# Vision block on one core: the expert mask as a VectorE product with choices spread by DMA, and filters made a period ahead

## The reference

```python
y = relu(bn(conv1_w · x)); wdyn = conv2_w · y + conv2_b      # 9 filter values per pixel
h = sum_k unfold3x3(x)[k] * wdyn[k]                          # (b, h*w, c)
n = layernorm(h); Q, K, V = n Wq + bq, n Wk + bk, n Wv + bv
h = h + softmax(Q K^T / 8) V
n = layernorm(h); idx = argmax(n router_w^T + router_b)      # one of 32 experts per token
hid = relu(n W1[idx] + b1[idx])                              # 16 wide
h = h + relu(hid W2[idx] + b2[idx])
```

## Time and profile before

| what | us |
|---|---|
| median of three runs | 1156.71 |
| lowest, highest | 1154.79, 1158.39 |
| profiled execution, its own time | 1155.53 |
| its span from first to last instruction | 1153.6 |
| TensorE busy in the span | 1108.8 |
| ScalarE busy | 630.7 |
| VectorE busy | 491.2 |

### The profile page before, as it was taken

One profiled execution on the slowest core, in us unless ns is written; L12 is line 12 of the kernel. 1 busy time (PEld: TensorE's weight loads), 2 busy tenths in 40 slices (PEclk: granted clock), 3 DMA queues, 4 the chain that ended last, 5 costly groups with the idle time before them and its releaser, 6 DMA issues.

```text
span 1153.6 us, 29604 instructions
## 1 busy us (share of the span) xinstructions
PE 1108.8 (96%) x12890; PEld 632.6 (55%) x12890; DVE 491.2 (43%) x1101; ACT 630.7 (55%) x698; POOL 11.2 (1%) x34
## 2 busy tenths in 40 slices
PE   6597999999999999999999999999999999999996
PEld 2132576666654565665656566555655555555542
DVE  6788726437255280724526272552503030311323
ACT  2355465564646465564656556564655645555551
POOL 3000000000000000000000000000000000000000
PEclk9999899999999999999999999999999999999997
DMA  5645323131105220041202121040000000000000
GB/s 149 139 111 129 78 65 68 30 74 29 47 12 117 53 66 2 14 93 38 65 11 59 38 65 39 11 94 10 11 2 11 2 11 1 11 1 11 2 2 20
DMA packets 15349, 51.67 MB, mean 45 GB/s; under 512 B 2846, under 2 KB 6046, under 8 KB 14828
## 3 DMA queue, kind: packets, MB, share of 16 engines
q1 hardware_dynamic: 15212, 49.68, 18.5%
HBM read 41.77 MB, written 4.75 MB: 40 GB/s over the span
## 4 chain that ended last, share of the span: by engine, by line
PE 93%; DVE 2%; DMA 2%; issue 1%; ACT 1%; SPq 0%; DVEq 0%
PE z_ps L664 39%; PE scores L653 37%; PE both L620 4%; PE both L635 4%; PE both L512 2%; PE both L616 1%; DMA filter_ring<-filters 1%; PE both L643 1%; PE both L550 1%; PE both L560 1%; DMA xin<-x_dram 1%; PE both L581 1%; PE both L600 1%; PE both L591 1%; PE both L627 0%
## 5 line engine op out<-in xcount | busy, mean ns | idle before, releaser
L856 ACT ACTIVATE probs<-scores 128x1024 f32<-128x1024 f32 x480 | 465.4, 1021 | 427.2 <-PE scores L653 427.2
L653 PE MATMUL scores<-g_t,keys_t 64*64 64x512 f32 x4096 | 528.7, 593 | 9.8 <-issue 8.5
L664 PE MATMUL z_ps<-probs,keys 64*64 64x512 f32 x4096 | 525.7, 592 | 0.0
L653 PEld LDWEIGHTS scores<-g_t,keys_t 64*64 64x64 f32 x4096 | 251.7, 134 | 209.4 <-issue 179.1
L664 PEld LDWEIGHTS z_ps<-probs,keys 64*64 64x64 f32 x4096 | 234.9, 134 | 158.7 <-issue 136.5
L1107 DVE COPY o_sb<-both 128x512 f32<-128x512 f32 x14 | 9.7, 691 | 322.6 <-PE both L635 322.6
L1007 DVE TENSOR_TENSOR hres<-hres,tap_product 128x504 f32<-128x504 f32 (+1 forms) x128 | 88.9, 694 | 11.2 <-issue 0.9
L1002 DVE SCALAR_TENSOR_TENSOR tap_product<-filter_ring,w,xin 128x504 f32<-128x504 f32 (+1 forms) x120 | 89.0, 742 | 7.0 <-DMA filter_ring<-filters 3.6
L620 PE MATMUL both<-y_t,w 64*64 64x512 f32 x464 | 66.9, 597 | 0.0
L849 ACT ACTIVATE hidden<-both 128x1024 f32<-128x1024 f32 (+1 forms) x58 | 58.5, 1009 | 6.5 <-PE both L620 6.5
L635 PE MATMUL both<-hidden,w 64*64 64x512 f32 x448 | 57.3, 592 | 0.0
(11 more groups left out here) (136 smaller groups left out, 589.8 us busy)
## 6 DMA issues: line engine op xcount, KB each, us to landing
filter_ring<-filters SPq DMA_DIRECT2D x90, 384.0 KB, 5.1
out_dram<-out_sb SPq DMA_DIRECT2D x32, 128.0 KB, 2.4
xin<-x_dram SPq DMA_DIRECT2D x6, 528.0 KB, 9.8
g_t<-g_t SPq DMA_DIRECT2D x24, 128.0 KB, 4.6
hidden<-once_dram SPq DMA_DIRECT2D x1, 930.0 KB, 14.5
hidden<-once_dram SPq DMA_DIRECT2D x1, 576.0 KB, 6.3
filters<-filters_sb SPq DMA_DIRECT2D x30, 18.0 KB
xin<-x_dram SPq DMA_DIRECT2D x1, 384.0 KB, 6.5
```

The source lines that it names most:

```text
L653: last = T.matmul(scores[rows_of(h), c, r * 512:(r + 1) * 512], keys_t[rows_of(r), i // NQ % 2, k * 128 + 64 * h:k * 128 + 64 * h + 64], g ...
L664: last = T.matmul(z_ps[rows_of(c), h, :], keys[rows_of(h), i // NQ % 2, 2 * k + r, :], probs[rows_of(h), (2 * g + c) % RING, r * 512:(r + ...
L856: A.activation(probs[:, unit % RING, :], scores[:, c, :], ACT.Exp, scale=SCALE if n else first_scale[:, 0:1]).then_inc(probs_ready, 1)
```

## The change

Blocks 3 to 13 (`CHOSEN_BY_DMA`, eleven blocks) no longer have the four mask matmuls of each `hid` fill. SyncE stores the turned one-hot (`onehot_t`, bf16) to HBM, waits for it, and loads it back with each expert's row repeated for its 16 hidden rows, as four DMAs to `chosen`. VectorE drains the `hid` fills with one operation on 128x1024: max(place, 0) times `chosen`. ScalarE does not touch them. The layernorm of block i becomes a fill of its own, `ln`; in usual periods it stands in group 7, after `lg`. `ot` moves from 10 to 8, `xt` from 8 to 9, `g` from 9 to 10, `hid0` to `hid3` to 12 to 15 and `o2` to 16. `cc` and `cv` of a pair come one period earlier (block 9's in groups 4 and 16 of period 3; 11, 13 and 15 in periods 5, 7 and 9), and SyncE's order changes with them.

```diff
-NONE = ("sum", "pow", "aw", "part", "z")
+NONE = ("sum", "ln", "pow", "aw", "part", "z")
+CHOSEN_BY_DMA = range(3, BLOCKS - 2)
 def fourth_groups():
-    return {..., 4: at(7, "sum2"),
+    return {..., 4: [*at(9, "cc"), *at(7, "sum2 ln")],
-            14: at(2, "hid3"), 15: at(2, "o2")}
+            14: at(2, "hid3"), 15: at(2, "o2"), 16: at(9, "cv")}
 def usual_groups(n):
-    pair = {4: at(j, "cc"), 7: at(j, "cv")} if j in PAIRED else {}
-    groups = merged({-1: at(m, "z"), 1: at(m - 1, "fin"), 2: at(m, "pz"), 4: at(i, "sum2"), 5: at(m, "yt"), 6: at(m, "lg")}, pair,
-                    {8: at(i, "xt"), 9: at(i, "g"), 10: [*at(m, "ot"), *at(j, "sum0 sum1")]})
-    if n < BLOCKS - 1:
-        return merged(groups, {11: at(m, "hid0"), 12: at(m, "hid1"), 13: at(m, "hid2"), 14: at(m, "hid3"),
-                               15: at(m, "o2")})
+    pair = {4: at(j + 1, "cc"), 7: at(j + 1, "cv")} if j + 1 in PAIRED else {}
+    groups = merged({-1: at(m, "z"), 1: at(m - 1, "fin"), 2: at(m, "pz"), 4: at(i, "sum2"), 5: at(m, "yt"),
+                     6: at(m, "lg"), 7: at(i, "ln")}, pair,
+                    {8: at(m, "ot"), 9: at(i, "xt"), 10: [*at(i, "g"), *at(j, "sum0 sum1")]})
+    if m in CHOSEN_BY_DMA:
+        return merged(groups, {12: at(m, "hid0"), 13: at(m, "hid1"), 14: at(m, "hid2"), 15: at(m, "hid3"), 16: at(m, "o2")})
+            def spread_choices(i):
+                ot = f"ot@{i}"
+                sp.wait_ge(drained[places.of[ot]], places.nth[ot])
+                for c in range(2):
+                    sp.dma_start(choices[i, :, c, :], onehot_t[64 * c:64 * c + E, :]).then_inc(choices_stored, 16)
+                sp.wait_ge(choices_stored, 32 * (i - CHOSEN_BY_DMA[0] + 1))
+                for f in range(FT):
+                    rows = choices[i, f * 128 // H:(f + 1) * 128 // H, :, :].rearrange("e c n -> e (c n)")
+                    sp.dma_start(chosen[:, f, :, :].rearrange("p c n -> p (c n)"),
+                                 rows.unsqueeze(1).broadcast_to([128 // H, H, 2 * 512])
+                                 ).then_inc(choices_loaded, 16)
                 if n > 3:
                     store_block(n - 2)
+                if n == 2:
+                    store_filters(NQ + 3)
                 if n + NQ + 1 < BLOCKS:
-                    if n > 1 and n + NQ + 1 in PAIRED:
-                        store_filters(n + NQ + 1)
-                    spread_filters(n + NQ + 1)
+                    spread_filters(n + NQ + 1, range(CHUNKS - 1))
+                if n > NQ and n + NQ + 2 in PAIRED:
+                    store_filters(n + NQ + 2)
+                if n - 1 in CHOSEN_BY_DMA:
+                    spread_choices(n - 1)
+                if n + NQ + 1 < BLOCKS:
+                    spread_filters(n + NQ + 1, range(CHUNKS - 1, CHUNKS))
                 if n + NQ < BLOCKS:
                     copy_queries(n + NQ)
                 if n in (2, 3):
                     store_block(n - 2)
+                if n == 3:
+                    store_filters(NQ + 5)
     # TensorE, hid fill
-                            T.matmul(mine[rows_of(c), r, :], mask_w[rows_of(r), cols[c]], onehot_t[rows_of(r), :],
-                                     start=True, stop=False)
+                            if i not in CHOSEN_BY_DMA:
+                                T.matmul(mine[rows_of(c), r, :], mask_w[rows_of(r), cols[c]], onehot_t[rows_of(r), :],
+                                         start=True, stop=False)
     # VectorE
+                if name == "ln":
+                    layernorm(i)
+                    return
+                if name.startswith("hid") and i in CHOSEN_BY_DMA:
+                    f, k = int(name[3:]), places.of[full]
+                    dve.wait_ge(choices_loaded, 16 * FT * (i - CHOSEN_BY_DMA[0] + 1))
+                    dve.wait_ge(filled[k], places.nth[full])
+                    V.scalar_tensor_tensor(hidden[:, f, :, :], place[k][:, :, :], 0.0, chosen[:, f, :, :], ALU.max,
+                                           ALU.mult).then_inc(drained[k], 1)
```

More of the change, by code:

```diff
@@ L108, in opening_groups @@
              *at(0, "pow3 pow4 pow5"), *at(3, "cv"), *at(0, "xt g")],
-        0: at(1, "sum0 sum1 sum2"),
+        0: at(1, "sum0 sum1 sum2 ln"),
         3: at(1, "xt"),
-        4: [*at(1, "g"), *at(2, "sum0 sum1 sum2")],
-        HALF: [*at(0, "part"), *at(3, "sum0 sum1 sum2")],
+        4: [*at(1, "g"), *at(2, "sum0 sum1 sum2 ln")],
+        HALF: [*at(0, "part"), *at(3, "sum0 sum1 sum2 ln")],
         10: at(2, "xt"),
@@ L133, in third_groups @@
 def third_groups():
-    return {-1: at(1, "z"), 0: at(0, "lg"), 2: at(0, "ot"), 3: at(1, "pz"), 4: [*at(0, "hid0"), *at(6, "sum2")],
+    return {-1: at(1, "z"), 0: at(0, "lg"), 2: at(0, "ot"), 3: at(1, "pz"), 4: [*at(0, "hid0"), *at(6, "sum2 ln")],
             5: at(0, "hid1"), 6: at(0, "hid2"), 7: at(0, "hid3"), 8: at(1, "yt"), 9: at(0, "o2"), 10: at(1, "lg"),
@@ L140, in fourth_groups @@
 def fourth_groups():
-    return {-1: at(2, "z"), 0: at(1, "hid2"), 1: at(1, "hid3"), 2: at(2, "pz"), 3: at(1, "o2"), 4: at(7, "sum2"),
+    return {-1: at(2, "z"), 0: at(1, "hid2"), 1: at(1, "hid3"), 2: at(2, "pz"), 3: at(1, "o2"), 4: [*at(9, "cc"), *at(7, "sum2 ln")],
             5: at(2, "yt"), 6: at(2, "lg"), 7: at(1, "fin"), 8: at(7, "xt"), 9: at(7, "g"),
             10: [*at(2, "ot"), *at(8, "sum0 sum1")], 11: at(2, "hid0"), 12: at(2, "hid1"), 13: at(2, "hid2"),
-            14: at(2, "hid3"), 15: at(2, "o2")}
+            14: at(2, "hid3"), 15: at(2, "o2"), 16: at(9, "cv")}
 def usual_groups(n):
     m, i, j = n - 1, n + NQ, n + NQ + 1
-    pair = {4: at(j, "cc"), 7: at(j, "cv")} if j in PAIRED else {}
-    groups = merged({-1: at(m, "z"), 1: at(m - 1, "fin"), 2: at(m, "pz"), 4: at(i, "sum2"), 5: at(m, "yt"), 6: at(m, "lg")}, pair,
-                    {8: at(i, "xt"), 9: at(i, "g"), 10: [*at(m, "ot"), *at(j, "sum0 sum1")]})
-    if n < BLOCKS - 1:
-        return merged(groups, {11: at(m, "hid0"), 12: at(m, "hid1"), 13: at(m, "hid2"), 14: at(m, "hid3"),
-                               15: at(m, "o2")})
+    pair = {4: at(j + 1, "cc"), 7: at(j + 1, "cv")} if j + 1 in PAIRED else {}
[4 more added lines that the diff above has]
+        return merged(groups, {12: at(m, "hid0"), 13: at(m, "hid1"), 14: at(m, "hid2"), 15: at(m, "hid3"), 16: at(m, "o2")})
     return groups
@@ L199, in vit_block_kernel @@
     filters = nc.dram_tensor("filters", (BLOCKS, HH, TAPS, BT * W), F32).ap()
+    choices = nc.dram_tensor("choices", (BLOCKS, E, 2, 512), BF16).ap()
     plan = whole_plan()
@@ L236, in vit_block_kernel @@
         onehot_t = sb("onehot_t", [128, 512], BF16)
+        chosen = sb("chosen", [128, FT, 2, 512], BF16)
         hidden = sb("hidden", [128, FT, 2, 512])
@@ L362, in store_filters, with spread_filters @@
                                      ).then_inc(filters_stored, 16)
-            def spread_filters(i):
+            def spread_choices(i):
[9 more added lines that the diff above has]
+                                 ).then_inc(choices_loaded, 16)
+            def spread_filters(i, parts=range(CHUNKS)):
                 sp.wait_ge(filters_stored, filters_stored_with(i))
-                for part in range(CHUNKS):
+                for part in parts:
                     slot, before = slot_of(i, part)
@@ L620, in fill @@
                             last = T.matmul(mine[rows_of(c), r, :], w1[rows_of(r), cols[c]], y_t[rows_of(r), :],
-                                            start=False, stop=True)
+                                            start=i in CHOSEN_BY_DMA, stop=True)
                     last.then_inc(done, 1)
@@ L1059, in drain @@
                             filters_used[slot] if t == CHUNK - 1 else None)
-                    if part == CHUNKS - 1:
-                        layernorm(i)
                     return
```

3 lines of the change are left out of this document (2 added, 1 removed).

## The result

In six runs each on one chip the changed kernel has a median of 1146.47 us (1142.41 to 1149.97), the kernel before 1155.75 (1153.89 to 1158.39): a ratio of 0.992, interval 0.9896 to 0.9944, or 6.5 to 12.0 us. Faster by 0.8%, as forecast. Measured again in another job, with 6 runs against 11, the same file gave 0.991 (0.9891 to 0.993).

A forecast was written before the change was run, and what follows sets the result against it. TensorE's steps were taken to bound the middle periods. Mask -9.5, `o2` +0.7, `xt` +0.6 and `cv` +0.5 sum to -7.7, so 1147.8 from 1155.53, forecast as 1148.0 us, range 1145 to 1152.5.

The forecast's parts named there:

- The mask: Mask matmuls removed from TensorE's 44 hidden fills in eleven blocks, 0.216 us each, all on the path: -9.5 us.
- ScalarE's drains at 0: 44 x 1.02 us of drains taken off ScalarE lie beside TensorE's work: price 0.
- The product at 1.23 us: VectorE's added 128x1024 product takes 1.23 us, bounds 1.02 and 2.45; 54 us more on VectorE, hidden beneath TensorE.
- `o2`'s wait: `o2` in group 16 waits for `hid3`'s drain: 1.69 against 1.72 just fits; 0.06 x 11 = +0.7 us, ends 0 and 13.
- The choices at price 0: Store and loads on SyncE land 10 us after `ot` is drained, before `hid0` needs them; cover 5.4 us: price 0.
- `xt`: `xt` waits 0.12 us behind VectorE's layernorm in periods 4, 6, 8, 10, 11: +0.6 us, ends 0 and 5 x 0.5.
- `cv` of block 9: In group 16 of period 3, `cv` waits for VectorE to drain `o2` of block 2: +0.5 us, once.
- Filters a period ahead at 0: Filters made a period earlier end VectorE's wait of 7.13 us, which TensorE didn't notice: gain 0 in the middle.
- The rival of late choices: TensorE waits at `hid1` if choices land beyond 15.4 us after `ot`'s drain; at 20 us, 1197; chance 0.05.
- The clock rival: Each new short wait drops TensorE's clock, next two steps at half speed, eleven blocks lose 38 us: 1184; chance 0.02.
- the 5 us at the top of the range: Allowance in the forecast's upper end for each `o2` waiting 0.3 us, with `xt` and `cv` at their ends.
- the cases that gain: The forecast itself, chance 0.78, and more than the sum, where none of the tight places holds: 1146, chance 0.06.

The follow-up runs named there:

- e1: The kernel before with only the mask matmuls of blocks 3 to 13 left out, so the output leaves out the choice: 1146.28 us, ratio 0.9931.
- e3: The changed kernel with VectorE's product on `hid3` issued twice in each of the eleven blocks: 1158.73 us in its one run.
- e4: The changed kernel with the four choices loads made twice, first into an unused tile, so the choices land later: 1179.7 us in its one run.
- the second profile: A second profile of the same changed kernel, run again unchanged: 1146.62 us (6 runs), ratio 0.991 to the kernel before.
- e6_xt_later: The changed kernel with `xt` in group 10, `g` in 11, and `cv` of block 9 ahead of `o2` of block 2: 1146.71 us, ratio 0.9904.
- e2: The changed kernel's schedule and filters, but masks on TensorE, drain on ScalarE and no choices by DMA: 1157.56 us, ratio 1.001 to the kernel before.
- e5: The changed kernel with `cc`, `cv` and the filter stores back where they were before: 1164.09 us, ratio 1.0064 to the kernel before.

## Why the prediction was right, point by point

**The mask: right.** -9.5 against -9.33 by e1 over the same eleven blocks, and 0.86 a period.

**ScalarE's drains at 0: right.** ScalarE's 44.8 us less moved nothing; e1 keeps its drains and has the same periods 12 to 14 as the changed kernel.

**The product at 1.23 us: right,** with 1.225 in the group above. I had taken it from the SBUF row of 1.226, against the estimate of 1.19 by the Trainium skill (VectorE: DVE Perf Modes, the TRN2 errata section). The trace speaks against that figure: with an operand from PSUM and one in bf16 the operation still takes what the SBUF row takes.

**`o2`'s wait: +0.7 charged, 0.2 measured.** The working was right to a few hundredths: 1.69 against 1.72 in it, and 0.34 + 1.22 + 0.15 = 1.71 in the trace. VectorE did start some hundredths later, and ten of the eleven periods still have no wait. e3 shows that there is 0.1 us of room and no more: made to wait, `o2` follows the product by 0.05, not 0.15. Period 5's 0.23 is a term that the prediction did not have: VectorE's pause, 0.4 us in front of the product.

**The choices at price 0: right, with less room than I wrote.** The cover of 15.4 us is 16.4 by e4 in periods with `xt` and `g`, 0.6 of it because `ot` is drained by the very next ScalarE instruction and not behind two others (the store goes out 1.9 us after `ot` starts, where I had 2.5). The rest is mostly how it is read: a wait in the trace counts from a modelled end, some 0.2 us late, and TensorE follows the product by 0.05 in e4 where I had 0.15. The 10 us held only where nothing else was on the queues. In period 12, SyncE's queue and the windows of its loads (columns as in the earlier trace rows):

```profile
883.61 0.78 SPq L375 DMA_DIRECT2D choices<-onehot_t  x2
886.45 2.54 SPq L380 DMA_DIRECT2D chosen<-choices  x4
```

```profile
889.00:892.00 3.00, 3.00 (x32) 1.68 (x28) 0.00 (x0) 1.50 (x3) 0.00 (x0) 1.00 0.50 192
892.00:895.00 3.00, 3.00 (x32) 1.68 (x28) 0.00 (x0) 1.87 (x2) 0.00 (x0) 1.00 0.24 91
```

Over half of the 1 MB moves at 192 GB/s and the rate has fallen by 892 to 895, some 10 us after the store. In period 4 a third filter chunk, the query copy and an image follow on the same queue:

```profile
353.44 0.78 SPq L375 DMA_DIRECT2D choices<-onehot_t  x2
355.37 2.57 SPq L380 DMA_DIRECT2D chosen<-choices  x4
358.65 1.49 SPq L393 DMA_DIRECT2D filter_ring<-filters  x2
361.89 1.34 SPq L403 DMA_DIRECT2D g_t<-g_t  x2
363.28 1.25 SPq L349 DMA_DIRECT2D xin<-x_dram  x2
```

```profile
368.28 1.22 DVE L1102 SCALAR_TENSOR_TENSOR hidden<-both,chosen 128x1024 f32<-128x1024 f32 x1 [4.50 <-DMA chosen<-choices]
```

There it takes 14.8 us from the store to the first product, VectorE waits 4.50, and some 1.5 us of the cover are left. In the second profile the product of that period starts at 14.5 and waits for TensorE, not for the DMA. I had named the image and the query copy as things queued behind the choices, and not asked whether they would slow what stands in front of them. The term stayed at 0, but "cover 5.4 us" was true of the late periods only.

**`xt`: +0.6, measured about 1.0.** The sum had 5 x 0.12. It was 0.09 in p6 and 0.06 in p11, near the charge, and 0.43 and 0.41 in p8 and p10, near the upper end of 0.5 but not for the reason given (logits late). It is VectorE's pause of 0.45 us without a releaser, which falls into the layernorm there (618.10 and 749.38). The kernel before has such pauses too (269.63 and 634.94 among others), and had no step waiting on them. The upper bound covered the size; I had read no row of it.

**`cv` of block 9: +0.5, measured 0.5.** TensorE after, with the last weighing of period 3, `cv`, and the first score step of period 4:

```profile
316.38 0.60 PE L693 MATMUL z_ps<-probs,keys 64*64 64x512 f32 x2
...
318.62 1.09 PE L588 MATMUL both<-conv,conv_w 64*64 64x512 f32 x8
320.51 1.95 PE L682 MATMUL scores<-g_t,keys_t 64*64 64x512 f32 x16 [0.81 <-issue]
```

The weighing starts at 316.38, so `cv` could have started at 318.10 and did at 318.62. The 0.81 behind it, with "issue", belongs to the loss at the start of period 4 that the other kernels have too. That loss is 1.7 us here, `cv`'s 0.5 included, and 1.4 in the kernel before, so period 4 as a whole is only 0.3 over before's; with `cv` ahead of `o2` it is 0.6 (e6_xt_later).

**Filters a period ahead at 0: the step that was wrong in kind.** As long as one asks what the move gives to the kernel before, it is 0, which e2 shows. But in this change its task is another. With the filters where they were, the choices' store queues behind the filter loads, and e5 loses 17.5 us. I had the line in hand, "the first two chunks now go out before `spread_choices` can hold them", and looked only at what the choices delay, not at what delays them. The rival of late choices named its point, 15.4 us, rightly. It took twice 10 us as its case, at 4.6 us a block; period 8 of e5 has 20.0 and 4.57 (its store goes out 1.1 us late, behind the filters' issues, which takes up the wider cover). What kept the rival from happening was this part of the change.

**The clock rival: a real mechanism that the changed kernel's waits don't set off.** Its waits of up to 0.5 us in front of fills left the granted clock at 1.00, in periods 10 and 11 among others (the windows above). Given waits of some 2 us and more at `hid1`, it is there: ten waits of 1.97 to 6.52 us in e4 and e5, seven falls. I had weighed it at 2 in 100 on the strength of one wait of 1.64 us without a fall, and that reading held. The Trainium skill (TensorE: Matmul & The Clock Gate, the second HAM failure mode) tells of small idles between groups that bring a fall; none came after waits of 1.32 us or less here.

**The sum.** -7.7 forecast; -7.9 by the distances up to period 15 in both profiles, -7.6 and -8.9 to TensorE's last instructions, and -9.3 between the medians, whose interval (-6.5 to -12.0) holds them all. That the small errors cancel, 0.5 too much for `o2` and 0.4 too little for `xt`, is luck. Two slips in the working changed nothing: the 5 us at the top of the range should be 6.3 by its own terms (3.3 + 2.5 + 0.5), and the chances of the cases that gain, 0.78 + 0.06, make less than the 0.85 given to faster.

## What to carry to other kernels

Where one engine is busy throughout, price a change by what leaves that engine, and then walk each new neighbour pair: here a distance of one step (1.72 us) held a drain that ends at 1.56 with 0.1 to spare, and a pause of 0.4 us on the draining engine was enough to break it once. A part of a change that is worth nothing to the old kernel can be what lets the new part work, so ask of every new transfer what is already in its queue, and take the part out to see. And compare by distances between repeated steps before believing a span: here 4.8 of 13 us were chance in the opening.

## What the runs showed of the hardware that I had not expected

- A store of 2 x 32 KB lets the loads behind it go 1.9 us after its issue in most periods (2.4 to 2.8 in two of the changed kernel's, up to 3.8 in other runs), and 6.7 to 8.4 us after it behind four loads of 384 KB issued just before on the same queue (e5).
- VectorE stands for about 0.45 us at fixed places of its program, with no releaser in the profile, in both kernels, and 82 of 85 such pauses have an instruction packet on DMA queue 14 beside them. That it is the cause is not shown. It costs only where a step waits for VectorE: 0.4 us in periods 8 and 10, 0.2 in period 5.
- The clock doesn't follow the length of a wait alone. It fell after waits of 2.00, 2.33, 2.36, 2.42, 2.67, 4.57 and 6.52 us, and not after 1.97, 2.50 and 2.70, nor after 1.32 and less. A fall cost about as much again as a wait of 2 us: 2.36 became 4.3 and 2.42 became 4.7, 4.57 became 6.9.
- At the start of period 4 TensorE loses 0.6 to 1.7 us in the four kernels compared above, part of it "issue" in the profile. Not explained; with `cv` moved ahead of `o2` 1.7 became 0.6.
